# GpSimd makes all parts of queries and keys; ScalarE writes the mask of every fourth head

## The reference

```
Q, K, V = q @ wq + bq, k @ wk + bk, v @ wv + bv     # 16 heads of 16 columns
att = einsum('bhqd,bhkd->bhqk', Q, K)
att = where(mask == 0, -1e9, att)
out = einsum('bhqk,bhkd->bhqd', softmax(att), V)
x  <- layer_norm(x + out @ wo + bo)
```

## Time and profile before

| | us |
|---|---|
| median of 3 runs | 1326.63 (1325.15 to 1328.39) |
| profiled execution | 1332.05, span 1330.3 |
| TensorE busy, whole span | 1171.1 (88%) |
| VectorE, ScalarE, GpSimd busy | 788.0, 634.3, 544.7 |
| attention of this layer, about | 66 to 434 us of the span |

### The profile page before, as it was taken

The page is one execution under the profiler, slowest core; times in us unless marked ns, Lnnn a source line. Parts: engine busy times, 40 slices in busy tenths (PEclk is TensorE's granted clock), DMA queues, the critical chain, the costliest instruction groups (busy, mean ns, idle before and its releaser), DMA issues. The chain is left out here.

```text
span 1330.3 us, 27248 instructions
## 1 busy us (share of the span) xinstructions
PE 1171.1 (88%) x8333; PEld 938.3 (71%) x8333; DVE 788.0 (59%) x3030; ACT 634.3 (48%) x1537; POOL 544.7 (41%) x850
## 2 busy tenths in 40 slices
PE   4599999999998999989999999834799986899996
PEld 3356666666654788779999999821576654789995
DVE  4678788888883378875433334256778875523231
ACT  2268787887877322233333333211567564333331
POOL 3334545454534334545333333222555543333331
PEclk9889999999999999999999999965899998899998
DMA  4857685545420891113222222156555597511110
GB/s 104 183 117 167 133 176 117 110 107 108 105 55 2 282 306 48 31 45 41 38 41 35 39 40 33 25 124 132 146 112 112 113 286 226 195 31 48 41 36 5
DMA packets 114934, 136.19 MB, mean 102 GB/s; under 512 B 23179, under 2 KB 101401, under 8 KB 110076
## 3 DMA queue, kind: packets, MB, share of 16 engines
q1 hardware_dynamic: 99560, 105.29, 33.3%
q0 software_dynamic: 15232, 29.17, 9.6%
HBM read 100.28 MB, written 35.18 MB: 102 GB/s over the span
## 5 line engine op out<-in xcount | busy, mean ns | idle before, releaser
L851 DVE CUSTOM_DVE_ANT_0 att_masked_scores<-att_S,Bm 128x256 bf16<-128x256 f32 x512 | 190.3, 418 | 42.6 <-PE att_S L593 29.3
L726 ACT ACTIVATE att_PT<-att_T 128x512 f32<-128x512 f32 x256 | 146.3, 591 | 52.9 <-PE att_T L615 49.0
L2566 ACT ACTIVATE moe_hT<-moe_H,moe_b 128x128 f32<-128x128 f32 x312 | 88.9, 369 | 170.3 <-PE moe_H L2479 163.7
L2491 PE MATMUL moe_Z<-moe_W,moe_hT 128*128 x624 | 141.6, 380 | 0.8 <-DVE moe_z L2791 0.8
L2654 POOL DMA_INDIRECT x<-Y,X x39 | 63.5, 1629 | 155.6 <-DVE Y L2802 150.9
L2491 PEld LDWEIGHTS moe_Z<-moe_W,moe_hT 128*128 128x128 f32 x624 | 115.6, 190 | 15.4 <-issue 1.2
L593 PE MATMUL att_S<-L_KS,L_QS 96*128 96x256 bf16 x512 | 99.4, 276 | 24.0 <-DMA L_KS<-att_k_dram 16.3
L1653 ACT ACTIVATE X<-out_T,L_b 128x128 f32<-128x128 f32 x184 | 52.7, 367 | 103.6 <-PE out_T L1459 103.6
L1932 DVE TENSOR_REDUCE out_mx<-out_S 128x2 f32<-128x512 f32 x128 | 84.9, 685 | 28.6 <-PE out_S L1330 26.6
L615 PE MATMUL att_T<-L_QS,L_KS 99*128 99x256 bf16 x512 | 97.9, 274 | 4.2 <-ACT att_T L731 3.9
L2791 DVE TENSOR_TENSOR moe_z<-moe_Z,moe_b 128x256 f32<-128x256 f32 x39 | 16.5, 424 | 142.4 <-PE moe_Z L2491 142.4
(11 more groups left out here) (473 smaller groups left out, 2516.2 us busy)
## 6 DMA issues: line engine op xcount, KB each, us to landing
moe_W<-in_L_ffn_W SPq DMA_DIRECT2D x16, 1024.0 KB, 13.4
L_W<-in_L_ffn_W POOLq DMA_DIRECT2D x12, 1024.0 KB, 16.8
att_q_dram<-att_pq SPq DMA_DIRECT2D x16, 384.0 KB, 4.0
att_k_dram<-att_pk SPq DMA_DIRECT2D x16, 384.0 KB, 2.8
L_QS<-att_q_dram SPq DMA_DIRECT2D x16, 384.0 KB, 4.9
L_KS<-att_k_dram SPq DMA_DIRECT2D x16, 384.0 KB, 8.0
L_QS<-att_q_dram SPq DMA_DIRECT2D x16, 256.0 KB, 5.5
L_KS<-att_k_dram SPq DMA_DIRECT2D x16, 256.0 KB, 8.6
```

Of the source, the lines that this page charges most:

```text
L726: nc.scalar.activation(PT[:, h % 8, :], bankT[h % 2][:, :], ACT.Exp).then_inc(exp_done, 1)
L851: ins = nc.vector.tensor_tensor_reduce(masked_scores[:, h % 2, u, :], bankS[h % 2][:, u * SEQ:(u + 1) * SEQ], masks[m // B][0][:, u * SEQ: ...
L2491: ins = nc.tensor.matmul(bankZ[:, 0:D], eT[:, s % 2, f * P:(f + 1) * P], w2e[:, f, :], start=(f == 0), stop=(f == NF - 1))
L2566: ins = nc.scalar.activation(eT[:, s % 2, g * P:(g + 1) * P], bankH[half][:, f * P:(f + 1) * P], ACT.Relu, bias=b1[:, bass.ds(e * NF + g, 1)])
```

## The change

Three things are changed. GpSimd makes the two bf16 copies of units 3 to 15 itself, between its subtractions; ScalarE keeps them for units 0 to 2. ScalarE copies the mask for heads 0, 4, 8 and 12 too (all but the very first head), into bank T0, right after the exponential of heads 14, 2, 6 and 10, with a semaphore of its own. TensorE leaves the mask matmul out for these heads and waits for that semaphore. Heads 2, 6, 10 and 14 keep the matmul.

```diff
+        fourth = lambda m, h: h % 4 == 0 and h + m > 0
+        fourth_no = lambda m, h: 4 * m + h // 4
...
-                if h % 2 and (m, h) != (0, 1):
+                on_mask = h % 2 and (m, h) != (0, 1) or fourth(m, h)
+                if fourth(m, h):
+                    pe.wait_ge(fourth_seeded, fourth_no(m, h))
+                elif on_mask:
                     pe.wait_ge(seeded, seed_no(m, h))
                 else:
                     pe.wait_ge(exp_done, H * m + h + 1)
...
-                nc.scalar.activation(bankT[1][:, :], masks[layer][1][:, :], ACT.Copy).then_inc(seeded, 1)
+                nc.scalar.activation(bankT[h % 2][:, :], masks[layer][1][:, :], ACT.Copy).then_inc(seeded if h % 2 else fourth_seeded, 1)
...
-                        if h % 2 and (b, h) != (M - 1, H - 1):
+                        if (h % 2 or h % 4 == 2) and (b < M - 1 or h < H - 2):
                             seed(b, h)
...
-                        if h == 1:
+                        if h == 1 and b < 0:
                             first_part(b + 3, 0)
-                        if h == 3:
+                        if h == 3 and b < 0:
                             second_part(b + 3, 0)
...
+            def first_part(m, side):
+                f, parts, at = ((fq, pq, q_place), (fk, pk, k_place))[side]
+                pool.wait_ge(*taken(("q", "k")[side], m))
+                if m >= 1:
+                    pool.wait_ge(spread[side], 16 * m)
+                nc.gpsimd.tensor_copy(flat(parts[:, at[0], :, :]), f[:, :]).then_inc(part1[side], 1)
+
+            def second_part(m, side):
+                r, parts, at = ((rq, pq, q_place), (rk, pk, k_place))[side]
+                pool.wait_ge(rest1[side], m + 1)
+                nc.gpsimd.tensor_copy(flat(parts[:, at[1], :, :]), r[:, :]).then_inc(part2[side], 1)
+
             def parts(m, side):
+                if m >= 3:
+                    first_part(m, side)
                 rest(m, side)
+                if m >= 3:
+                    second_part(m, side)
                 third_part(m, side)
```

More of the change, by code:

```diff
@@ L476, in attention_pipeline @@
         ot_out, rec_done = sem("ot_out"), sem("rec_done")
-        seeded = sem("seeded")
+        seeded, fourth_seeded = sem("seeded"), sem("fourth_seeded")
         ybb_done, moments0, root_step0, rooted0 = sem("ybb_done"), sem("moments0"), sem("root_step0"), sem("rooted0")
@@ L616, in scores_T @@
                                            QS[0:ROWS_ALL, m % 3, h, :], start=False, stop=(u == NU - 1),
-                                           skip_group_check=h % 2 == 1 and (m, h) != (0, 1))
+                                           skip_group_check=bool(on_mask))
                 ins.then_inc(st_ready, 1)
@@ L755, in _ @@
                             keys(b + 3)
-                        if h == 5:
+                        if h == 5 and b < 0:
                             first_part(b + 3, 1)
-                        if h == 7:
+                        if h == 7 and b < 0:
                             second_part(b + 3, 1)
```

## The result

The changed kernel takes 1343.45 us (median of 4 runs, 1341.22 to 1345.77) against 1326.34 us before: ratio 1.0122, 95% interval 1.0100 to 1.0144, so 13 to 19 us slower. The forecast was 1334.3 us with a range of 1321 to 1343. The direction came out as forecast, the size did not: +17.1 us and not +7.7.

A forecast was written before the change was run, and what follows sets the result against it. A chain of exponential, mask copy and score through ScalarE was taken to bound the short stretches, whatever TensorE saves. 3.0 us for earlier beats plus 4.7 for the last two, +7.7 on 1326.63, gave 1334.3 us, range 1321 to 1343.

The forecast's parts named there:

- T6 to T8: Short stretch between starts of the transposed scores of heads 6 and 8: forecast 1.98 to 1.90 us, -0.08 a beat.
- The lateness of exponential 6: On ScalarE, key bank copy, mask 7 and output copy make exponential 6 start about 0.19 us late; an estimate.
- the limit of 0.85: One GpSimd copy must stay under about 0.85 us so the key side ends before VectorE's normalisation starts.
- slower by GpSimd: Rival, chance 0.10: at 1.16 us a copy, the key side holds VectorE's normalisation; +9.5 us more, 1344 us.
- The long stretches keep their work: they held no mask that goes.: Stretches between the short ones, holding a projection and a quad's values, were forecast unchanged in steady beats.
- the steady part: Four short stretches change by +0.23, -0.08, -0.05 and +0.18 us: +0.28 a beat, +1.7 us over six beats.
- exponential 3 and mask 5: Come about 0.5 us later; the 1.7 us projection before head 5's score covers that, except in the last two beats.
- T14 to T0: Short stretch from head 14's transposed score to the next beat's head 0: forecast 1.53 to 1.71 us, +0.18.
- Beats 0 to 5, 12 and 13: Beats 0 to 5 +0.8 us, partly hidden in transfer waits; beat 12 +0.5; beat 13 keeps its time.
- same: Rival, chance 0.15: steady beats level or better, beat 13's half clock disappears giving up to 1.5 us; about 1328.6 us.
- The last two beats: No projection covers the 0.5 us delay; eight stretches lose 3.40 + 0.47 + 0.82 = +4.7 us.
- a half clock: TensorE's clock halving in the last two beats, where it idles more, would add 2 to 4 us to the forecast.

The follow-up runs named there:

- Parts alone: Against the kernel before: GpSimd makes the part copies, while the masks stay with TensorE; 1327.45 us, ratio 0.9989 (0.9973 to 1.0006).

## Why the prediction was right and wrong

**Right: the direction and its mechanism.** What TensorE saves is worth nothing where it then waits for exponential, mask copy and score one after the other. The chain of 0.42 + 0.63 + 0.66 = 1.71 us was measured as 1.70 to 1.71 at head 4 and head 12 in every steady beat, T6 to T8 as 1.87 (forecast 1.90). The lateness of exponential 6, an estimate, was real.

**Right: GpSimd.** A copy took 0.61 to 0.67 us against the forecast 0.65 and the limit of 0.85. Timeline of GpSimd, then of VectorE's normalisation, changed kernel:

```profile
275.90 0.61 POOL L791 CAST att_pk<-att_fk 128x512 bf16<-128x512 f32 x1
276.59 1.16 POOL L778 TENSOR_TENSOR att_rk<-att_fk,att_pk 128x512 f32<-128x512 f32 x1
277.82 0.67 POOL L796 CAST att_pk<-att_rk 128x512 bf16<-128x512 f32 x1
278.56 1.16 POOL L783 TENSOR_TENSOR att_pk<-att_rk,att_pk 128x512 bf16<-128x512 f32 x1
...
280.68 0.71 DVE L237 TENSOR_SCALAR att_z<-att_z,att_mv,att_r 128x256 f32<-128x256 f32 x2
```

The key side ends at 279.72, 0.96 us before the normalisation, which takes its free 0.71 us. Parts alone confirms that the copies cost nothing. The rival "slower by GpSimd" was named at 1344 us, next to the result, but it is not what happened.

**Wrong: "The long stretches keep their work: they held no mask that goes."** True of TensorE's work, and the step asked no more. ScalarE's copies at heads 6 and 10, which free the shared bank for the projections of the long stretches, stand right behind the new masks. Before, they ended 0.23 and 0.47 us ahead of the projections, less than the 0.54 us that a mask takes up. That is 0.18 + 0.23 = 0.41 us a beat, nearly the whole miss of the steady part (+0.74 and not +0.28 a beat; beats 6 to 11 +4.5 and not +1.7 us). The step's own question, what is queued behind the added instruction and who waits for that, was put for exponential 3 and mask 5 and not for these two copies. The run with the copies first shows it: both long stretches back at the values of before.

**Wrong by a little: T14 to T0.** 1.79 and not 1.71 us, since TensorE's second wait at head 0 stands between the mask's wait and the score; the run with the order turned gives 1.71.

**Beats 0 to 5, 12 and 13.** Forecast +0.8 us together. Beats 1 and 4 alone lost 1.9 to 2.1, the steady loss and, in beat 1, a longer T8 to T10. In the others the transfer wait hides the loss as forecast: 118.5 and 115.0 us before, 119.1 and 114.2 after. Beat 12 lost 0.52 and 0.50 us, as forecast (+0.5). Beat 13, which was to keep its time, became 0.5 us shorter (20.60 and 20.53 before, 20.08 and 20.09 after), and the half clock that stood in it in both traces of before is in neither of the changed kernel: the rival "same" had named this, at up to 1.5 us.

**The last two beats: +4.7 forecast, +5.4 and +4.8 measured.** The chain part was right: beat 14 +2.15 where 2.3 was expected. Beat 15 holds what the rivals had named and the sum had left out, a half clock. After waits of 0.44 and 1.24 us for masks TensorE's granted clock is 0.52 from 431.40 to 434.50, in the main at 1.2 GHz. In the second trace the drop came at head 6 of that beat, after waits of 0.80 and 0.76 us, and with TensorE's own masks there was none. If the chain cost 2.35 us there, half of the forecast 4.7, the clock cost the rest, an estimated 0.9 and 0.3 us, and not the 2 to 4 that the rivals gave it.

**The sum.** 7.7 us forecast, 12.2 found in stretches that repeat, 17.1 (13.3 to 19.1) and 14.6 (11 to 20) timed. The place of the remaining 2 to 5 us stays open, and it may be noise in part: 12.2 lies inside the second interval and 1.1 us under the first, and the spans of the four traces differ by 12.5 us on average (1330.3 and 1322.4 before, 1341.1 and 1336.5 after). Two traces of one kernel differ by 3.5 us in the transfer beats and 3 us behind the attention, so more traces would be needed to see it. The profile of before, which the sum started from, lay 5.4 us over its own median.

**Moving the masks to the other heads** did what the chain says (no wait on a mask, T8 to T10 0.22 us shorter) and met a bound that the busy shares of the earlier trace rows did not show. VectorE is busy 82% of the beat, but it works in order, and for two or three heads of each beat its maxima are the last thing the scores wait for.

## What to carry to other kernels

When an instruction is added to an engine's queue, list every instruction behind it up to the next idle time and who waits for each, the bank copies for other stages too, and not the chain alone for which it was added. Hand work from the engine that bounds to a helper only where something else lies between the helper's input and its use: with the part copies on GpSimd, such masks cost 15 to 17 us in the short stretches and nothing measurable in the long ones. And take two traces before a difference of a few microseconds is divided up: two of the same kernel were 7.9 us apart in span.

## What the hardware showed that was not expected

- Small VectorE operations wait out a GpSimd subtraction whole. att_MQ on 128x32 takes 0.19 us alone and 1.17 us when it starts 0.03 us after one; two normalisations take 0.71 us alone and 0.94, 1.70 and 2.65 us beside one or two, and end within 0.2 us of GpSimd's operation. In "SBUF — State Buffer", section Who interferes with whom, the Trainium skill gives this as an exclusive lock on a shared pair of ports, for VectorE operations with two SBUF inputs and for single-input ones in a two-port mode; the rows of att_MQ, with two inputs in SBUF, agree. The normalisation has one such input and was held too, as the rule has it for a two-port mode; in which mode it ran no trace shows. Maxima, whose scores come from PSUM, kept their 0.42 us beside the same subtractions. The kernel before had this hold as well: there an att_MQ operation takes 1.12 to 1.18 us in ten of 16 beats, and ends 0.05 us after the subtraction.
- A GpSimd conversion of 128x512 from float32 to bfloat16 takes 0.61 to 0.67 us, about half of a subtraction with two inputs (1.16).
- TensorE's granted clock was 0.50, 0.63 and 0.52 in three brief windows, each with a part at 1.2 GHz: at 384 us before and at 157.4 us in the changed kernel, both in beats where the scores of head 8 had waited for a transfer, and at 431.4 us, where a score had waited 1.24 us for a mask. A drop in beat 15 came only with the added waits. A wait alone does not bring it: in beats 3 and 5 of the kernel before these scores waited 2.70 and 1.96 us, and the clock stayed at 1.00.
